# Out-projection by token tiles with the gate's columns in its operand, running sums of the expert picks, and place one-hots on Pool

## The reference

```
h  = concat(patches(x) @ W.T + b, (weight_l @ weight_r)[x_txt])
q, k, v = layernorm(h) @ W_q, W_k, W_v            # 16 heads of 64
a  = sigmoid(layernorm(h) @ W_gate + b_gate)
S_t = a_t * S_(t-1) + k_t v_t ;  o_t = q_t S_t     # scan over the 68 tokens of a sequence
h  = h + concat_heads(o) @ W_o
z  = layernorm(h)
p  = softmax(z @ Wg) over 8 experts; the top 2, their weights divided by their sum
h  = h + sum over a token's 2 experts of weight * (relu(z @ W1[e] + b1[e]) @ W2[e] + b2[e])
```

## Time and profile before

| | |
|---|---|
| median of 3 runs | 389.65 us (386.09 to 389.90) |
| the profiled execution | 388.81 us, of which the span in the trace is 387.0 us |
| first projection begins | 39.00 us |
| out-projection begins | 204.46 us |
| first transposition of a gathered row (the experts' start) | 273.16 us |
| last expert block on PE ends, about | 365 us |
| mean granted clock of PE, as a share of 2.4 GHz | 0.951 |

### The profile page before, as it was taken

One profiled execution on the slowest core, in us unless ns is written; L12 is line 12 of the kernel. 1 busy time (PEld: TensorE's weight loads), 2 busy tenths in 40 slices (PEclk: granted clock), 3 DMA queues, 4 the chain that ended last, 5 costly groups with the idle time before them and its releaser, 6 DMA issues.

```text
span 387.0 us, 7120 instructions
## 1 busy us (share of the span) xinstructions
PE 349.3 (90%) x2545; PEld 300.2 (78%) x2546; DVE 218.8 (57%) x333; ACT 115.2 (30%) x255; POOL 142.5 (37%) x147
## 2 busy tenths in 40 slices
PE   4989999999999999999799999698799999999800
PEld 3765999999999999999797887474588888888700
DVE  1056898758586858697730254676354545545216
ACT  1035453353435342423212111430132323232300
POOL 5632025241315132411403995005435656554310
PEclk9999999999999999999959999978999999999955
DMA  7920006022020300000008700030212221222165
GB/s 206 304 82 0 2 4 216 3 87 91 3 97 2 95 2 2 2 2 2 1 2 328 327 0 0 2 116 5 65 43 76 73 69 68 69 68 55 42 205 181
DMA packets 12093, 28.95 MB, mean 75 GB/s; under 512 B 2144, under 2 KB 6752, under 8 KB 11552
## 3 DMA queue, kind: packets, MB, share of 16 engines
q1 hardware_dynamic: 9632, 21.99, 16.1%
q0 software_dynamic: 2432, 6.56, 5.8%
HBM read 23.17 MB, written 5.37 MB: 74 GB/s over the span
## 4 chain that ended last, share of the span: by engine, by line
PE 67%; issue 9%; POOL 8%; DMA 6%; DVE 6%; SPq 1%; ACT 1%; POOLq 0%; DVEq 0%
PE ps L798 10%; PE ps L549 7%; PE ps L565 7%; PE ps L428 7%; PE ps L429 6%; PE ps L430 6%; POOL w1lo L1539 5%; PE ps L777 3%; PE ps L779 3%; PE ps L778 3%; PE ps L788 3%; PE ps L525 3%; DMA pt<-patches 2%; POOL w1hi L1537 2%; PE ps L526 2%
## 5 line engine op out<-in xcount | busy, mean ns | idle before, releaser
L428 PE MATMUL ps<-xnhi,wlo 128*128 128x272 f32 x192 | 57.1, 297 | 0.9 <-DVE xnlo L1136 0.9
L1161 DVE RECIPROCAL invU<-U 128x272 f32<-128x272 f32 x32 | 57.6, 1827 | 0.0
L429 PE MATMUL ps<-xnlo,whi 128*128 128x272 f32 x192 | 55.5, 289 | 0.0
L430 PE MATMUL ps<-xnhi,whi 128*128 128x272 f32 x192 | 55.3, 288 | 0.0
L1037 ACT ACTIVATE hr<-ps,b 128x128 f32<-128x128 f32 x96 | 27.4, 369 | 78.6 <-PE ps L788 75.9
L1486 POOL TENSOR_TENSOR qA<-qraw,invU 128x544 f32<-128x544 f32 x16 | 22.4, 1402 | 70.8 <-DVE invU L1161 36.0
L798 PE MATMUL ps<-w,hr 128*128 x192 | 45.2, 379 | 0.0
L1559 POOL DMA_INDIRECT yrows<-yb,scatter_u x24 | 24.6, 1023 | 40.3 <-DVE yb L1401 34.7
L428 PEld LDWEIGHTS ps<-xnhi,wlo 128*128 128x128 f32 x192 | 36.1, 188 | 2.4 <-issue 1.7
L1168 DVE TENSOR_TENSOR pb<-ps,causal 128x592 uint32<-128x592 uint32 (+3 forms) x32 | 27.3, 854 | 18.9 <-PE ps L549 18.6
L798 PEld LDWEIGHTS ps<-w,hr 128*128 128x128 f32 x192 | 34.7, 190 | 3.8
(11 more groups left out here) (176 smaller groups left out, 607.8 us busy)
## 6 DMA issues: line engine op xcount, KB each, us to landing
w<-w SPq DMA_DIRECT2D x1, 4096.0 KB, 14.7
wraw<-w_attn SPq DMA_DIRECT2D x8, 384.5 KB, 3.3
w<-w SPq DMA_DIRECT2D x6, 512.0 KB, 4.1
yin<-yrows SPq DMA_DIRECT2D x4, 384.0 KB, 5.1
wv<-w_v SPq DMA_DIRECT2D x4, 256.0 KB, 2.8
wo<-w_o SPq DMA_DIRECT2D x1, 1024.0 KB, 13.0
w<-w SPq DMA_DIRECT2D x1, 1024.0 KB, 5.2
b<-b SPq DMA_DIRECT2D x1, 1024.0 KB, 16.7
```

Of the source, the lines that this page charges most:

```text
L428: pe.matmul(dst, slo, mhi[n], start=(i == 0), stop=False)
L429: pe.matmul(dst, shi, mlo[n], start=False, stop=False)
L430: last = pe.matmul(dst, shi, mhi[n], start=False, stop=(i == len(pairs) - 1))
L1161: dve.reciprocal(invU[:, g * GT:(g + 1) * GT], U[:, g * GT:(g + 1) * GT]).then_inc(s_a, 1)
```

## The change

The out-projection is turned round: `out_part(r, a0, a1)` takes a tile r of 128 tokens as weights (oT) and streams wo, so its output has tokens on partitions and needs no transposition. hT is added by two matmuls with shifted identities (own), and wo gets 8 more columns between its two halves, the product of each head pair's rows of W_o with the centred gate, so that one output of 264 columns holds the sum h and its gate logits. This product is made at the start of the program by `gate_of_heads` from a transposed copy of W_o (w_ot, a new 1 MB input, held in oT until attention writes it), on PE after keep_warm, which goes from 7 matmuls to 3; DVE copies it into wo (keep_gate_of_heads). The first seven head pairs of tiles 0 to 3 are placed between the scores and mixes of the last pair.

For each tile DVE takes mean and variance (bn_stats, bn_aggr), the top 2 of the unnormalised logits, the pick, and a running sum of picks (prev); ACT writes the normalised row and the plain row from PSUM. `count(r)` gets the tokens ahead by 2 to 4 small matmuls; `find_places` has DVE work out places for two tiles at a time. POOL makes 16 of the 18 one-hots, times the row number; DVE makes the last two. The softmax weights are worked out after block 2 of the experts (`weigh`). xrows holds each token twice, once a pick, and is written in 18 DMAs instead of 4. w1 is loaded in full during attention, w1hi is made on ACT between the last copies of attention, and POOL begins w1lo there. Pool's constants are made before its first split of weights, and four memsets on DVE move to behind the second xnlo.

```diff
-            sp.dma_start(wo[:], w_o).then_inc(s_wo, 16)
...
+            sp.dma_start(wot, w_ot).then_inc(s_wot, 16)
+            for m in range(DC):
+                o = m * (P + E)
+                sp.dma_start(wo[:, :, o:o + P], w_o[:, :, m * P:(m + 1) * P]).then_inc(s_wo, 16)
...
+                for e in (hp - 1,) if hp < HP - 1 else (hp - 1, hp):
+                    sp.dma_start(w1[:, e], w_1[:, e]).then_inc(s_w1, 16)
...
+            for r in range(RT):
+                sp.wait_ge(s_norm, r + 1)
+                p0 = DUP if r == RT - 1 else 0
+                for i in range(PICKS):
+                    at = i * TOK + token0(r)
+                    sp.dma_start(xrows[at + p0:at + P], xrow[p0:P, r]).then_inc(s_xrows, 16)
+            sp.wait_ge(s_xrows, 16 * PICKS * RT)
...
+            def gate_of_heads():
...
+                for a in range(HP):
+                    for m in range(DC):
+                        last = pe.matmul(ps[:, 2, (1 + a) * E:(2 + a) * E], wot[:, 2 * m + a // 4, a % 4 * P:(a % 4 + 1) * P],
+                                         own[:, m, P * (1 - m):P * (1 - m) + E], start=(m == 0), stop=(m == DC - 1))
+                last.then_inc(s_wogmm, 1)
...
-            keep_warm(7, 7)
+            keep_warm(3, 7)
+            gate_of_heads()
...
+            def out_part(r, a0, a1):
...
+                for a in range(a0, a1):
+                    last = pe.matmul(ps[:, bank, 0:OW], oT[:, a, tok], wo[:, a, :], start=(a == 0), stop=(a == HP - 1))
+                    for m in range(DC if a == 0 else 0):
+                        pe.matmul(ps[:, bank, m * P:m * P + P + E], hT[:, m, tok], own[:, m, :], start=False, stop=False)
+                if a1 == HP:
+                    last.then_inc(s_op, 1)
...
-            for g in range(G):
-                pair_scores(HP - 1, 1, g, bank=4 + 2 * (g % 2))
-                if g:
...
+            out_part(0, 0, HP - 1)
+            pair_scores(HP - 1, 1, 0)
+            out_part(1, 0, HP - 1)
+            mix(HP - 1, 1, 0, bank=6)
+            pair_scores(HP - 1, 1, 1)
...
+            pair_scores(HP - 1, 1, 3)
+            out_part(3, 2, HP - 1)
+            mix(HP - 1, 1, 3, bank=7)
...
+            def count(r):
+
+                pe.wait_ge(s_pick, r + 1)
+                if r >= 1:
+                    pe.wait_ge(s_prev, r)
+                if r >= 2:
+                    pe.wait_ge(s_ranked, r - r % 2)
...
+                n = PICKS if r < RT - 1 else PICKS + 1
+                if r > 0:
+                    add(ones_m, prev[:, r:r + 1].to_broadcast([P, n, E]), 0, n, True)
+                add(tri, pick[:, r], 0, PICKS, r == 0)
+                if n > PICKS:
+                    all_of(r, 1, PICKS, n)
+                all_of(r, 0, 1, n, stop=True).then_inc(s_count, 1)
...
+            for r in range(4):
+                out_part(r, HP - 1, HP)
+            out_part(4, 0, HP)
+            count(0)
+            count(1)
+            out_part(5, 0, HP)
+            count(2)
+            count(3)
...
+            pe.wait_ge(s_hrow, 4)
+            keep_warm(1, 3)
+            count(8)
...
-                last = pe.matmul(ps[:, 6, 0:NB], at_place[:, a, :], entry[:, a], start=(a == 0), stop=(a == A - 1))
+                if a < A - PICKS:
+                    pe.wait_ge(s_place, a + 1)
+                else:
+                    pe.wait_ge(s_last, a - A + PICKS + 1)
+                last = pe.matmul(ps[:, 6, 0:NB], at_place[:, a, :], in_block[:, a], start=(a == 0), stop=(a == A - 1))
             last.then_inc(s_tabmm, 1)
-            keep_warm(5, 3)
+            keep_warm(4, 3)
...
+            def split_expert(e):
+
+                act.activation(w1hi[:, e], w1[:, e], ACT.Copy).then_inc(s_w1hi, 1)
...
+            split_expert(0)
             evacuate_o(HP - 2, G - 1)
+            split_expert(1)
+            split_expert(2)
...
+            def normalise_of(r):
+                act.wait_ge(s_shift, r + 1)
+                act.activation(xrow[:, r].rearrange("p (c n) -> p c n", n=P), summed(r), ACT.Identity, bias=shift[:, r:r + 1],
+                               scale=rstd_r[:, r:r + 1]).then_inc(s_norm, 1)
+
+            def keep_row(r):
+                act.activation(hrow[:, r].rearrange("p (c n) -> p c n", n=P), summed(r), ACT.Copy).then_inc(s_hrow, 1)
...
+            def centre_gate():
...
+                for m in range(DC):
+                    dve.tensor_copy(own[:, m, E * m:E * m + P], ident[:])
+                    last = dve.tensor_tensor(own[:, m, P * (1 - m):P * (1 - m) + E], wg[:, m, :], ps[:, 2, 0:E], ALU.subtract)
+                last.then_inc(s_own, 1)
...
+            def keep_gate_of_heads():
...
+                dve.tensor_copy(wo[:, :, LG], ps[:, 2, E:(1 + HP) * E].rearrange("p (a e) -> p a e", e=E)).then_inc(s_wog, 1)
...
+            centre_gate()
             normalise(0)
+            keep_gate_of_heads()
             split_stream(0)
...
+            def take_moments(r):
+                dve.wait_ge(s_op, r + 1)
+                link(dve.bn_stats(spread[r % 2][:], summed(r)))
+                dve.bn_aggr(moments[:, r], spread[r % 2][:]).then_inc(s_mom, 1)
+
+            def scale_of(r):
+                dve.wait_ge(s_std2, r + 1)
+                link(dve.reciprocal(rstd_r[:, r:r + 1], std[:, r:r + 1]))
+                dve.wait_ge(s_mom, r + 1)
+                dve.scalar_tensor_tensor(shift[:, r:r + 1], moments[:, r, 0:1], -1.0, rstd_r[:, r:r + 1],
+                                         ALU.mult, ALU.mult).then_inc(s_shift, 1)
+
+            def choose(r):
+                dve.wait_ge(s_op, r + 1)
+                link(dve.max(top[:, r, :], gated(r)))
+                link(dve.max_index(topi[:, r, :], top[:, r, :], gated(r)))
+                dve.tensor_tensor(pick[:, r], expert_no[:, r],
+                                  topi[:, r, 0:PICKS].unsqueeze(2).to_broadcast([P, PICKS, E]), ALU.is_equal
+                                  ).then_inc(s_pick, 1)
...
+                    dve.wait_ge(s_prev, r)
+                    dve.tensor_tensor(prev[:, r + 1], prev[:, r].bitcast(F32), pair_e[:], ALU.add).then_inc(s_prev, 1)
...
+            def find_places(r, n):
+                a = slice(PICKS * r, PICKS * (r + n))
+                dve.wait_ge(s_count, r + n)
+                dve.wait_ge(s_pick, r + n)
+                dve.tensor_tensor(rank_e[:, 0:PICKS * n], rank[:, a],
+                                  pick[:, r:r + n].bitcast(F32).rearrange("p r i e -> p (r i) e"), ALU.mult
+                                  ).then_inc(s_ranked, n)
+                dve.wait_ge(s_ranked, r + n)
+                link(dve.tensor_reduce(rank_f[:, a], rank_e[:, 0:PICKS * n], AX_X, ALU.add))
+                link(dve.tensor_scalar(high[:, a], rank_f[:, a], 0.5 - P / 2, P * 1.5 * 2.0 ** 23, ALU.add, ALU.add))
+                link(dve.tensor_scalar(high[:, a], high[:, a], P * 1.5 * 2.0 ** 23, None, ALU.subtract))
+                dve.tensor_tensor(place_of[:, a], rank_f[:, a], high[:, a], ALU.subtract).then_inc(s_rest, 1)
+                if r == RT - 1:
+                    dve.wait_ge(s_rest, RT // 2 + 1)
+                for i in range(PICKS if r == RT - 1 else 0):
+                    k = PICKS * r + i
+                    dve.tensor_scalar(at_place[:, k, :], place[:], place_of[:, k:k + 1], row_no[:, r, i:i + 1],
+                                      ALU.is_equal, ALU.mult).then_inc(s_last, 1)
...
+            def tile(r):
+                take_moments(r)
+                choose(r)
+                scale_of(r)
+                if r < RT - 1:
+                    add_up(r)
...
+            find_places(0, 2)
+            tile(4)
+            find_places(2, 2)
+            tile(5)
+            tile(6)
...
+            dve.wait_ge(s_count, RT)
+            link(dve.tensor_tensor(more[:], total, steps[:], ALU.is_gt))
+            link(dve.tensor_reduce(blocks[:, 1:1 + E], more[:], AX_X, ALU.add))
+            link(dve.tensor_tensor_scan(before[:], ones_e[:], blocks[:, 0:E], 0.0, ALU.mult, ALU.add))
+            find_places(RT - 1, 1)
+            link(dve.tensor_tensor(base_e[:], before[:].unsqueeze(1).to_broadcast([P, A, E]),
+                                   pick[:].bitcast(F32).rearrange("p r i e -> p (r i) e"), ALU.mult))
+            link(dve.tensor_reduce(base[:], base_e[:], AX_X, ALU.add))
+            link(dve.scalar_tensor_tensor(border[:], base[:], float(P), high[:], ALU.mult, ALU.add))
...
+            dve.tensor_scalar(gather_u[:], ps[:, 6, 0:NB], -1.0, 0.0, ALU.add, ALU.max).then_inc(s_tab, 1)
...
+                if b == 2:
+                    weigh()
...
-                pool.tensor_copy(w1hi[:, e], w1[:, e]).then_inc(s_w1hi, 1)
...
+            for a in range(A - PICKS):
+                r, i = a // PICKS, a % PICKS
+                if r % 2 == 0 and i == 0:
+                    pool.wait_ge(s_rest, r // 2 + 1)
+                pool.tensor_scalar(at_place[:, a, :], place[:], place_of[:, a:a + 1], row_no[:, r, i:i + 1],
```

(1 more changed line is left out.)

538 lines of the change are left out of this document (199 added, 339 removed).

## The result

The changed kernel took 371.94 us (median of 4 runs, 371.22 to 373.10) against 387.87 us for the kernel before on the same chip: ratio 0.967, 95% interval 0.960 to 0.974. The ratio compares the executions in the fast state alone, two of the four of the kernel before (386.09 and 383.50 us), so it is not the quotient of the medians, 0.959. The profiled execution took 371.22 us, 369.2 us of it span.

What follows compares the result with a forecast made beforehand. What counts was how early the last token's pick is known and how long the rest takes after it. From 388.8 us, 15.8 us less up to the experts (start's +3.3 included) and 0.4 more gave 373.4 us; range 371 to 376, chance 0.54.

Steps and rivals of the forecast that it cites:

- Start, +3.3 us: Program start: 1.6 us delay of the first projection behind the gate's product and copy, 1.7 us from a clock fall.
- Rival (a): Start is free: the gate's product is quicker or the clock stays up; 370.1 us, chance 0.13.
- Last pair: Last head pair's attention with the placed parts: 21.3 us of PE work, plus 1.7 us for a clock fall.
- Rival (b): Clock stays at half through the last pair, 5.0 us lost instead of 1.7; 376.7 us, chance 0.12.
- Tiles: Attention's end to last output, 215.5 to 240.9 us: 0.69 wait, 1.8 last matmuls, 19.9 whole tiles, 3.1 counts.
- DVE: Routing on DVE beside the out-projection: 2.3 to 2.4 us a tile, ending at 240.5 us, level with PE.
- Rival (c): DVE or Pool bounds: 378.2 us (DVE tiles), 377.4 (Pool one-hots) or 378.7 (queued small DMAs); chance 0.13.
- Rival (d): Slower than before: PE's counts wait for DVE tile by tile; at 5.0 us a tile 394 us; chance 0.03.
- Last output to experts: Last tile's output to first gathered block: 5.85 us to the table, 2.4 for it, 5.0 behind it, 13.25 in all.
- Pool: Pool's one-hots: 0.5 us each, between 0.2 and 1.6; the last four hidden behind 6 us of DVE.
- Rival (e): Last pair: the placed parts only lengthen it by their own 14 us; no separate chance given.
- The signs: Profile signs named beforehand as right (such as xnlo at 38.5 to 39.5 us) or wrong (such as Pool's one-hots over 1 us).

Runs made afterwards that it cites:

- gate_mixed: Changed kernel with the copy into wo behind the first xnlo and three keep_warm matmuls spread through the gate's product: 370.72 us, ratio 0.961.
- parts_after: Changed kernel with the out-projection parts of tiles 0 to 3 behind the last mix instead of between scores and mixes: 380.9 us, ratio 0.979.
- gate_then_warm: Changed kernel with gate_of_heads ahead of keep_warm(3, 7) on PE instead of behind it: 373.65 us, ratio 0.963.
- dve_more: Changed kernel with four extra linked bn_stats on DVE before that of each of tiles 0 to 7: 381.47 us, ratio 0.987.
- counts_last: Changed kernel with all counts behind the last tile's output on PE and all find_places behind the last choose on DVE: 379.8 us, ratio 0.981.
- wg_late: Changed kernel with wg's 8 KB DMA issued behind the second half of the patches instead of ahead: 373.25 us, one run.

## Why the prediction was right

The forecast was 373.4 us, inside 371 to 376; 371.94 us was measured, and the profiled execution, on which the sum was made, took 371.22 us. The 2.2 us between are 1.4 ahead of the experts (255.96 us against 257.4; 1.05 of it in the last pair, most of the rest behind the last output) and 1.0 behind them, less 0.2 around the span.

- **Start, +3.3 us.** The last mix of pair 6 begins at 194.65 instead of 191.37 us: 3.28. The sum is right and its parts are not, so that it fits this closely is luck. The 32 records took 0.113 us each, not 0.133, and xnlo began at 39.00 (39.15 predicted). Yet of the 1.43 us by which the first projection is late, 0.65 are already there at the variance matmuls (28.87 against 28.22 us), which I gave to nobody: "Wg's DMA goes ahead of the patches and is 8 KB: nothing that shows" failed. The fall came as predicted, for 3 us, and cost 1.4 instead of 1.7 us: the matmuls of the values begin 2.8 us late (46.38 against 43.59). Some 0.5 us more arise between there and pair 6, and I can't give them to one step. The four memsets vanish under the fall, as predicted. But then the fall is not worth its 1.4 us: without it (gate_mixed) PE waits for DVE instead, and only 0.5 us of it are gained up to pair 6. Rival (a), a free start, did not come: all ten traces with the 32 records in one run have the fall, and without it some 1.5 us against the kernel before remain in gate_mixed.
- **Last pair.** Predicted 21.3 us of work and one fall of 1.7; measured 22.2 us of work and no fall: the parts took 15.3 us instead of 14.1, scores and mixes 6.8 instead of 7.0. The fall is not a property of the kernel: with a wait of 1.84 to 1.86 us in this place it shows in seven of eleven traces (before, parts_after, gate_then_warm, dve_more, counts_last, gate_mixed, wg_late), and in none of the three that fill the wait, which chance alone would give about once in twenty. In the five of the seven that have the parts in place it lasted about 3.4 us, as predicted; in the two without them, before and parts_after, some 10 and 17 us. The prediction took a matter of chance for a step, and this step is the one that failed: 1.7 us were in the sum that no row of this execution has. Rival (b), half clock all through, needs the parts away: parts_after shows it.
- **Tiles.** From attention's end to the last output 25.5 us predicted, 25.36 measured. Here the working holds term by term: the wait took 0.66 us (0.69 predicted), the matmuls of the counts 3.2 (3.1), and those of the tiles the other 21.5 (1.8 and 19.9).
- **DVE.** "2.3 to 2.4 us" a tile failed: 1.64. I added the linked durations of one tile (the terms give 2.2, and were rounded up), but instructions that do not depend on each other start before the one ahead has ended: MAX8 begins at 221.61 us, bn_aggr at 221.51 and takes 0.18. "Level with PE" is therefore wrong, with 6.1 us to spare. Rival (c) keeps its size, because dve_more prices it: 3.0 us a tile is 1.36 more than 1.64, eight times that less 6.1 is 4.8 us, what the prediction had. Rival (d)'s turning point stays too, near 1.64 + (15.9 + 6.1) / 8 = 4.4 us a tile.
- **Last output to experts.** 5.60 us to the table (5.85 predicted), 2.18 for it (2.4), 5.07 behind it (5.0). The last is keep_warm at half clock, as assumed; at full clock it would have been the gather, 4.1 us.
- **Experts and end.** +0.4 us predicted, -0.6 measured; `weigh` costs nothing that shows.
- **Pool.** 0.78 us a one-hot lies between the bounds of 0.2 and 1.6, above the 0.5 taken; the last four end at 245.5 us, before the table at 248.7. All 16 took 0.78 to 0.81 us here. Rival (c)'s price for Pool fits these rows: at 1.6 us each the 16 would run from 227.15 to 252.8 us, 4 us past the table's start. The contention that the Trainium skill warns of ("GPSIMD Engine Reference", Key points: with VectorE instructions that read two inputs from SBUF) agrees with the one one-hot of counts_last that took 1.25 us beside in_block. In the changed kernel the one-hots are done before in_block begins, so it cost nothing here. Whether it also made the 1.61 us of the earlier trace rows, no run separates.
- **Small DMAs.** The 128 KB ones took 8.0 us each where 512 KB took 3.0, beside w2's 4 MB (DMA share 0.87 from 218 to 240 us); the last two, of 64 KB, took 2.0. No run separates their size from w2's traffic. No gather waited for them: the first is issued 0.8 us behind the end of gather_u, as before. The Trainium skill's rule of 1 MiB or more ("DMA: Bandwidth & Descriptors", Bandwidth) may describe their price, but nothing was waiting to pay it.
- **Rival (e)** falls with parts_after and counts_last: placed elsewhere, the same work costs 9 and 8 us more. Each of the two is about half of the gain; they were not taken away together, so whether they add up is not shown.
- **The signs.** Those named for being right came: xnlo at 39.00 us, a fall before 46 us, no idle PE in the last pair, the last output at 243.11 and the first gathered block at 255.96 us, every tile on DVE under 2.5 us. None of those for being wrong did.

## What to carry to other kernels

Ask first where a new piece of work lies: here the place of the out-projection's parts and of the routing was worth 9 and 8 us, while the engine of the one-hots was worth nothing. Count an engine's room as the chain that has to fit between two outputs, not as one minus its busy share, and take what a group of instructions costs from start to start. Where PE idles beside small matmuls the half clock can follow, in some executions and not in others; fill the wait with work that is due anyway, and give the fall a chance rather than a fixed price, and price it where the next engine's chain ends: at the start it cost 1.4 us at PE and 0.5 us further on.

## What the runs showed of the hardware

- After 32 records of 8-column matmuls in a row (3.6 us at full clock) the granted clock fell to 0.50 in each of ten traces that have them unbroken, with 0.8 to 1.6 us of idle time behind them or none. The fall at the start lasted about 3 us in some and over 5 us in others (wg_late: 0.50 from 40 to 44 us and 0.64 up to 46).
- At full clock 32 records of 8 columns took 3.63 us, 0.113 us each, and eight records of 512 columns 3.68 us, 0.46 each.
- Behind a wait of 1.84 to 1.86 us in the last pair the granted clock fell in seven of eleven traces and stayed in four.
- Small DVE instructions that wait for the one before stood 0.20 to 0.23 us apart, start to start, at 0.17 to 0.19 us each; those that don't, 0.08 to 0.12 us (bn_aggr and MAX8, 0.10). So the ten instructions of a tile took 1.64 us, where the sum with a link each gave 2.2.
- A one-hot of 128 elements took 0.78 to 0.81 us on POOL and 0.34 on DVE; beside a DVE instruction with two inputs in SBUF one took 1.25 us on POOL.
- The first gathered block was there 4.0 to 4.1 us behind the start of gather_u, in each of the five runs where PE was waiting for it.
